# The opening of a transformer block on one core: operand fills taken one by one, the second batch's normalised rows written by ScalarE, and the first slots' order written as a list

## The reference

```python
mod = (_silu(L0_c) @ L0_wmod).reshape(8, 6, 1, -1)      # sa, ca, ga, sb, cb, gb
ga, gb = sign(.) * maximum(abs(.), 0.25)
h = _layernorm(x) * (1 + ca) + sa
x = x + ga * attention(h)        # softmax(q k^T / 4) v, then wo, with biases
h = _layernorm(x) * (1 + cb) + sb
x = x + gb * ffn(h)              # shared: gelu(h up) down; routed: the same, times the gate of the top 4 of 16
```

## Time and profile before

| | us |
|---|---|
| median of 3 runs | 888.06 |
| lowest, highest | 887.6, 888.15 |
| the profiled execution | 887.85 |
| its span, first to last instruction | 886.1 |
| PE busy | 834.1 (94%) |
| ACT busy | 681.8 (77%) |
| DVE busy | 607.6 (69%) |
| POOL busy | 395.8 (45%) |

### The profile page before, as it was taken

How to read it: one execution, slowest core, us unless ns; L and a number is a source line. 1 busy time by engine, 2 the same in 40 slices (tenths; PEclk the granted TensorE clock), 3 DMA queues, 4 the chain that set the end, 5 groups by cost and what they waited for, 6 DMA issues and landing times.

```text
span 886.1 us, 19423 instructions
## 1 busy us (share of the span) xinstructions
PE 834.1 (94%) x7652; PEld 450.5 (51%) x7652; DVE 607.6 (69%) x1211; ACT 681.8 (77%) x1158; POOL 395.8 (45%) x349
## 2 busy tenths in 40 slices
PE   5858788999999999999999999999999999998998
PEld 4322133355545575566545655566555554555555
DVE  4675677777688866977588776976687668632452
ACT  5468878878997789878988889878987788855452
POOL 4365215224744255335633464426623263346472
PEclk9987889899999999999999999999999999999999
DMA  7024400344025221424025402431314300330140
GB/s 259 13 75 131 137 13 14 97 127 138 13 61 175 90 61 52 148 62 138 25 68 169 138 2 73 154 100 25 105 48 149 119 2 1 133 120 1 61 163 26
DMA packets 47290, 77.18 MB, mean 87 GB/s; under 512 B 6392, under 2 KB 41432, under 8 KB 43104
## 3 DMA queue, kind: packets, MB, share of 16 engines
q1 hardware_dynamic: 47200, 75.94, 27.1%
HBM read 63.47 MB, written 12.34 MB: 86 GB/s over the span
## 4 chain that ended last, share of the span: by engine, by line
PE 74%; ACT 9%; DVE 8%; POOL 4%; issue 3%; DMA 0%; ACTq 0%; DVEq 0%
PE scalar_bank L950 21%; PE down_bank L1118 18%; PE vector_bank L1026 9%; PE scalar_bank L1009 6%; PE vector_bank L1009 6%; PE vector_bank L950 5%; DVE neg_max L907 3%; PE scalar_bank L1038 3%; ACT q_aug L701 2%; ACT probs L715 2%; PE vector_bank L1050 2%; ACT rows L684 1%; DVE gelu L894 1%; ACT f_ring L673 1%; PE scalar_bank L1062 1%
## 5 line engine op out<-in xcount | busy, mean ns | idle before, releaser
L907 DVE TENSOR_REDUCE neg_max<-vector_bank 128x1 f16<-128x512 f32 x484 | 306.7, 686 | 84.9 <-PE vector_bank L1009 75.6
L715 ACT ACTIVATE probs<-scalar_bank 128x512 f32<-128x512 f32 x486 | 262.3, 605 | 41.9 <-PE scalar_bank L1009 39.2
L651 POOL TENSOR_TENSOR act_lo<-gelu,act_hi 128x512 f16<-128x512 f32 x144 | 172.7, 1217 | 164.9 <-ACT act_hi L692 146.8
L1118 PE MATMUL down_bank<-down_hi,act_hi 64*128 64x256 f16 x1120 | 174.8, 271 | 0.4 <-PE down_bank L1118 0.2
L1118 PE MATMUL down_bank<-down_lo,act_hi 64*128 64x256 f16 x1120 | 173.7, 269 | 0.0
L1118 PE MATMUL down_bank<-down_hi,act_lo 64*128 64x256 f16 x1120 | 173.7, 269 | 0.0
L1009 PE MATMUL vector_bank<-k_aug,q_aug 64*128 64x512 f16 x484 | 132.9, 393 | 13.9 <-ACT q_aug L701 7.4
L894 DVE TENSOR_TENSOR gelu<-gelu,gates 128x512 f32<-128x512 f32 x128 | 110.3, 882 | 47.7 <-ACT gelu L750 47.4
L1009 PE MATMUL scalar_bank<-q_aug,k_aug 64*128 64x512 f16 x486 | 126.3, 389 | 3.9 <-ACT probs L715 1.7
L750 ACT ACTIVATE gelu<-scalar_bank 128x512 f32<-128x512 f32 x144 | 85.0, 596 | 57.6 <-PE scalar_bank L950 39.0
L1026 PE MATMUL vector_bank<-probs,v_aug 128*32 128x512 f32 x992 | 117.0, 601 | 0.0
(11 more groups left out here) (200 smaller groups left out, 1255.2 us busy)
## 6 DMA issues: line engine op xcount, KB each, us to landing
gates<-gates_by_expert SPq DMA_DIRECT2D x32, 1024.0 KB, 5.2
q_aug<-q_parts SPq DMA_DIRECT2D x90, 64.0 KB, 2.7
k_aug<-k_parts SPq DMA_DIRECT2D x90, 64.0 KB, 3.1
x_pre<-in_x SPq DMA_DIRECT2D x8, 512.0 KB, 4.6
x_post<-in_x SPq DMA_DIRECT2D x8, 512.0 KB, 6.5
out<-x_post SPq DMA_DIRECT2D x16, 256.0 KB, 3.6
gates<-in_w_up SPq DMA_DIRECT2D x4, 576.0 KB, 11.2
gates<-in_w_down SPq DMA_DIRECT2D x4, 576.0 KB, 4.5
```

What stands on the lines that cost most here:

```text
L651: pool.tensor_tensor(act[1][:, c, :], gelu[:, n % NGELU, :], act[0][:, c, :], ALU.subtract).then_inc(s_elo, 1)
L715: scalar.activation(probs[:, n % U, :], src[:], ACT.Exp, scale=SCALE).then_inc(taken[kind], 1)
L907: dve.tensor_reduce(neg_max[:, (u // 2) % TT, at:at + 1], src[:], AX.X, ALU.max, negate=True).then_inc(done, 1)
L1118: ins = pe.matmul(o, act[a][at:at + 64, act_slot(b, c), tok:tok + P], wd[w][at:at + 64, c, :], start=n == 0 and k == 0, stop=c == NEX - 1 ...
```

## The change

Five things change.

1. `fill` becomes three items. `("fill", 0)` fills `q_aug[1]`, `("fill", 1)` `k_aug[1]`, `("fill", 2)` `v_aug[1]`. The fill of `v_aug[0]` goes into POOL's setup behind that of `k_aug[0]` and counts on `s_aug0`. The waits follow: the first batch's `qk_in` and `v` wait for `s_aug0` at 3 alone, the second batch's `qk_in`, `no_max` and `v` for `s_aug1` at 3.
2. The second batch's `rows1` moves from DVE to ACT: four activations with scale and bias. The bias (minus mean times the reciprocal deviation) is made by two more small instructions on POOL in `stats1`, with a semaphore `s_bias1` of its own.
3. `late` on DVE is cut in two: the weight split stays, the modulations and gates become an item `gm`.
4. The first 459 items of the list are written out in `BEGIN`, up to the maxima of the ninth slot; the rest keeps its order. The last 2222 items are the same in both lists. In `BEGIN` many of the pairs of `max` and `exp` are parted.
5. Within that, `mods` moves on SP from behind the first `qk_in` to the very front of the list, ahead of the second batch's `x_pre`. `gb` moves ahead by 17 places of SP's stream and `wsplit` 5 goes from ahead of `qk` (0, 1) to behind `pv` (2, 0).

```diff
+BEGIN = [("h1T", 0, 0, 0), ("mods", 0, 0, 0), ("h1T", 0, 1, 1), ("first", 0, 0, 0), ("x_pre", 1, 0, 0), ("first", 0,
+    1, 1), ("qk_out", 0, 2, 2), ("first", 0, 2, 3), ("max", 0, 0, 2), ("qk_out", 0, 3, 3), ("first", 0, 4, 4), ("max",
+    0, 3, 9), ("late", 0, 0, 0), ("qk_in", 0, 2, 2), ("max", 0, 10, 10), ("qk_in", 0, 3, 3), ("max", 0, 11, 11),
+    ("first", 0, 5, 5), ("stage", 0, 3, 3), ("qk", 0, 2, 2), ("gm", 0, 0, 0), ("max", 0, 12, 15), ("first", 0, 6, 6),
+    ("maxT", 0, 0, 0), ("qk", 0, 3, 3), ("max", 0, 16, 16), ("stage", 0, 4, 5), ("stats1", 1, 0, 0), ("max", 0, 17,
+    18), ("first", 0, 7, 7), ("exp", 0, 0, 1), ("max", 0, 19, 19), ("exp", 0, 2, 2), ("max", 0, 20, 21), ("fill", 0,
+    0, 0), ("max", 0, 22, 22), ("exp", 0, 3, 3), ("v", 0, 0, 0), ("wsplit", 0, 0, 0), ("exp", 0, 4, 4), ("v", 0, 1,
+    1), ("wsplit", 0, 1, 1), ("rows1", 1, 0, 0), ("exp", 0, 5, 5), ("max", 0, 23, 24), ("fill", 0, 1, 1), ("max", 0,
+    25, 25), ("stage", 0, 6, 6), ("exp", 0, 6, 6), ("max", 0, 26, 26), ("wsplit", 0, 2, 2), ("h1T", 1, 0, 0), ("exp",
+    0, 7, 7), ("max", 0, 27, 30), ("h1T", 1, 1, 1), ("exp", 0, 8, 8), ("wsplit", 0, 3, 3), ("qk_out", 1, 0, 0),
+    ("max", 0, 31, 31), ("maxT", 0, 1, 1), ("exp", 0, 9, 9), ("wsplit", 0, 4, 4), ("max", 0, 32, 32), ("exp", 0, 10,
...
+    begin = [(kind, n, b) for kind, b, first, last in BEGIN for n in range(first, last + 1)]
+    placed = set(begin)
+    return begin + [item for item in HEAD + parted([item for _, _, item in sorted(spots)]) if item not in placed]
...
                     if n == (2 if b == 0 else 0) and b < 2:
-                        sp.wait_ge(s_aug0, 2)
-                        sp.wait_ge(s_aug1, 4)
+                        sp.wait_ge((s_aug0, s_aug1)[b], 3)
...
+            pool.memset(v_aug[0][:], 1.0).then_inc(s_aug0, 1)
...
                 if kind == "fill":
-                    pool.memset(q_aug[1][:].bitcast(U32), 0).then_inc(s_aug1, 1)
-                    pool.memset(k_aug[1][:].bitcast(U32), 0x3C003C00).then_inc(s_aug1, 1)
-                    for m in v_aug:
-                        pool.memset(m[:], 1.0).then_inc(s_aug1, 1)
+                    dst, value = ((q_aug[1][:].bitcast(U32), 0), (k_aug[1][:].bitcast(U32), 0x3C003C00), (v_aug[1][:], 1.0))[n]
+                    pool.memset(dst, value).then_inc(s_aug1, 1)
...
                     power(b, mv[0], rstd[0], s_ln1, s_rs1)
+                    if b == 1:
+                        mean, var = mv[0][:, :, 0], mv[0][:, :, 1]
+                        pool.tensor_scalar(var, mean, -1.0, None, ALU.mult).then_inc(s_bias1, 1)
+                        pool.wait_ge(s_bias1, 1)
+                        pool.wait_ge(s_rs1, 4)
+                        pool.tensor_tensor(var, var, rstd[0][:], ALU.mult).then_inc(s_bias1, 1)
...
+                elif kind == "rows1" and b == 1:
+                    scalar.wait_ge(s_bias1, 2)
+                    wait(scalar, made["h1T"], 2, b, 0)
+                    for t in range(TT):
+                        scalar.activation(rows1[:, t, :], x_pre[:, t, :], ACT.Identity, bias=mv[0][:, t, 1:2],
+                                          scale=rstd[0][:, t:t + 1]).then_inc(s_ln1, 1)
...
                     w4_lo(1)
+                elif kind == "gm":
                     dve.wait_ge(s_setup_mm, 2)
...
-                elif kind == "rows1" and b > 0:
+                elif kind == "rows1" and b > 1:
...
-                        dve.wait_ge(s_aug1, 4)
+                        dve.wait_ge(s_aug0, 3)
+                        if b > 0:
+                            dve.wait_ge(s_aug1, 3)
```

More of the change, by code:

```diff
@@ L101 @@
 HEAD = [("x_pre", 0, 1), ("h1T", 0, 0), ("h1T", 1, 0), ("first", 0, 0), ("first", 1, 0), ("first", 2, 0), ("first", 3, 0)]
-EARLY = {("late", 0): 4.47, ("fill", 0): 14.82, ("first", 4): 3.2, ("first", 5): 5.04, ("first", 6): 9.23, ("first",
-    7): 16.56, ("qk", 2): 6.68, ("qk_out", 2): -4.56, ("qk", 3): 12.18, ("qk_out", 3): -1.18, ("qk_in", 2): 2.91,
-    ("qk_in", 3): 6.45, ("v", 0): 22.33, ("v", 1): 24.2, ("wsplit", 0): 22.13, ("wsplit", 1): 29.84, ("wsplit", 2):
-    32.78, ("mods", 0): 5.13, ("stage", 3): 3.59, ("stage", 4): 18.1, ("stage", 5): 29.04}
+EARLY = {("late", 0): 4.47, ("first", 4): 3.2, ("first", 5): 5.04, ("first", 6): 9.23, ("first", 7): 16.56, ("qk", 2): 6.68, ("qk_out", 2): -4.56, ("qk", 3): 12.18, ("qk_out", 3): -1.18, ("qk_in", 2): 2.91, ("qk_in", 3): 6.45, ("v", 0): 22.33, ("v", 1): 24.2, ("wsplit", 0): 22.13, ("wsplit", 1): 29.84, ("wsplit", 2): 32.78, ("mods", 0): 5.13, ("stage", 3): 3.59, ("stage", 4): 18.1, ("stage", 5): 29.04, ("fill", 0): 14.82, ("fill", 1): 17.82, ("fill", 2): 22.82, ("gm", 0): 6.47}
 SPLITS = [(0, 3), (0, 7), (0, 11), (2, 11), (3, 9)]
@@ L260, in plan @@
         slot(g, lambda place, *items: put(g, place, *items))
-    return HEAD + parted([item for _, _, item in sorted(spots)])
+    begin = [(kind, n, b) for kind, b, first, last in BEGIN for n in range(first, last + 1)]
+    placed = set(begin)
+    return begin + [item for item in HEAD + parted([item for _, _, item in sorted(spots)]) if item not in placed]
 PLAN = plan()
@@ L427, in block_kernel @@
         s_ln1, s_ln2 = sem("ln1_steps"), sem("ln2_steps")
+        s_bias1 = sem("second_ln1_bias")
         s_rs1, s_rs2 = sem("rstd1_steps"), sem("rstd2_steps")
```

50 lines of the change are left out of this document (added).

## The result

The changed kernel takes 891.56 us (median of 7 runs, 890.24 to 892.78) against 888.15: a ratio of 1.0035, 95% interval 1.0024 to 1.0046. It is slower by a third of a per cent where 1.0% faster was forecast. (888.15 is a median of seven too; one of those seven took 1640.13 us, far from every other run here.) Its profiled execution took 891.04 us with a span of 889.3 us, against 886.1 us of span before.

What follows compares the result with a forecast made beforehand. PE was taken as the bound, busy nearly throughout, so opening gains pass through as a shift. Head 6.1, setup 0.3, (a) 1.4 and (b) 1.2 make 9.0 us off 887.85: 879.0 us as median, range 869 to 886.

Steps and rivals of the forecast that it cites:

- Fills: Four POOL fills (5.49 us) leave the way ahead of the second batch's power; POOL has room, the `v` wait goes.
- Rows by ACT: Second batch's normalised rows move from DVE (4.19 us there) to ACT, at 2.35 us for four.
- The head, 6.1 us: Stretch from 47.40 us: ACT reaches `qk` (0, 1) at 69.5 instead of 75.65 us; lower bound 3.0 us gained.
- signs of being wrong: ACT waiting for the bias, DVE for `x_pre` at `stats1`, or a mean clock under 0.85 from 80 to 180 us.
- Setup: Opening: fewer maxima ahead of `first` 4 gain 0.3 us (0 to 0.6); two maxima ahead of the gates cost nothing.
- (a): Turn to the second batch: fewer maxima in a row and `exp` products under the wait gain 1.4 us (0 to 2).
- (b): PE's 1.60 us wait for the second norm's rows at 155.47 us shrinks: 1.2 us gained (0 to 1.6).
- (c): Slots around the first batch's `maxT` 2 and other turns: same sum of work and waits, 0 (-2 to +3).
- (d): Two half-clock stretches behind a `maxT`: 5.2 us would go at full clock, but new ones may come; taken as 0.
- Given back later: Rival, 18%: the head gains, but the finer order costs what (a) and (b) were to bring; 882.5 to 886.3 us.
- The clock too: Rival, 24%: shorter waits behind each `maxT` keep the clock full there; 869 to 876.5 us, most likely 874.
- Slower: Rival, 9%: parted `max` and `exp` make PE wait for banks in turn, doubling half-clock time; 891 us.

Runs made afterwards that it cites:

- list_to_second: The changed kernel's list, gates right behind the weight split, only up to the first batch's second `maxT`, old order behind: 881.85 us, ratio 0.9941.
- list_to_fifth: As list_to_second, but with the written-out list kept up to the second batch's first `maxT`: 889.26 us, ratio 1.001.
- fills_only: Old order, fills as single steps behind the second batch's power, gates right behind the weight split, rows still on DVE: 889.66 us, ratio 1.0018.
- gates_back: The changed kernel with one item moved, `gm` right behind `late`, ahead of `max` 10 and 11: 890.43 us, ratio 1.0025.

## Why the prediction was wrong, point by point

**Fills.** The step held for POOL (the `v` wait is gone, the fills found room), but alone it brought nothing, since DVE's rows then met the moved fill and the weight split.

**Rows by ACT.** Right, with its price: 2.06 us against 2.35. It carries the head.

**The head, 6.1 us.** The term was right in size and was reached only without the late gates: ACT came to `qk` (0, 1) 5.7 us earlier in list_to_second. In the changed kernel it came at 74.29, 1.4 us earlier, and the transposes at 60.12, not at 55 to 57. The load of `x_pre` was in time, and of the signs of being wrong that were named none came: the clock from 80 to 180 us was 0.93, not under 0.85.

**Setup.** The step that failed first: "its chain from 34.95 on holds the same instructions, so nothing". The same instructions in another order were not nothing. Two maxima went first, 1.9 us; the gates were then held beside POOL, 1.9 us; the four maxima behind the gates came late, and PE, which is in order, waited for them with a `first` product and the transposes of `maxT` 0 queued behind, and lost its clock. I had placed the gates' end at about 39 us; it was 42.4. Cost: 4.2 us at the first copies, 2.1 (the clock fell on `v` in both profiles) to 3.7 us (in neither) at the second.

**(a)** Right in size: 1.4 us alone against before, 0.95 us against slot C of list_to_second (15.29 to 14.34 us). But the clock then fell on the `v` products and took 2 us.

**(b)** Right: 1.2 forecast, 1.0 measured alone, the wait 0.34 us after.

**(c)** The step that failed most. "The same sum of work and of waits": 0, with -2 to +3. In the changed kernel it was a loss of 1.8 us in A and B (3.2 in list_to_fifth), 2.7 in D (5.6 alone), 1.6 in F and G. The sum of PE's work is not the same, because the score products had run two at a time: 159 turns for 132, and some 7.7 us more of PE's work over the eight slots. The code's `64 * (u % 2)` and the even pairs of the old list would have told it, and so would a look at the starts in PE's timeline. I had read only durations.

**(d)** Left at 0. In the whole the clock was better in the profile after (24.1 us at half clock instead of 37.6), but that paid for most of PE's added work only. Its place changes from execution to execution.

**The rivals.** "Given back later" has the right shape, with the ends set too near, as it let the small steps lose no more than (a) and (b) were to bring; its 882.5 to 886.3 do not even follow from the 3 to 6 us that it names, which give 882 to 885. "The clock too" came true by itself without its result. "Slower" had the right sign and time (891 us) by another mechanism: 14 us more of half clock were its condition, and there were 13 us less; what cost was PE's own work and the gates. It is in single slots (A, D) that a parted order and more half clock came together as it said; its waits did not, for PE's idle time there hardly changed. Its 9% were too few, for its mechanism was one of several by which a list of 460 places, each argued only at the few that looked bad, could lose.

The forecast was 9.0 us gained and 3.2 were lost in the profiled execution. Of the 12.2 us between, 4.5 are the setup (4.2 lost for 0.3 gained), none the head (6.1 in H, as forecast), 6.2 the slots A to G (3.6 lost where (a) and (b) were to gain 2.6), and 1.5 the late dip of the clock, of which the forecast had nothing.

By the experiments, the accounts close at the ninth copies: -5.6 for the list up to the second slot, +3.7 late gates, +1.8 for A and B, -1.6 for C, +2.7 for D, -0.9 for E, +1.6 for F and G give +1.7. These are leads of single profiles, with the chance said above. D of the changed kernel can be held against D of list_to_second, at nearly the same clock (0.92 and 0.91): of its 2.75 us more, 1.46 are PE busy (17.33 for 15.87) and 1.29 PE idle, beside waits of ACT for single products (seven, of 0.45 to 1.35 us each, between 122 and 133 us). No kernel was run that restores the pairs within the new slots, so that the parted pairs are the cause of PE's added work is argued from the starts, the count and the busy time, not shown by an experiment.

## What to carry to other kernels

Before reordering small products, look at their starts as well as their durations: two that start together share the array, and moving one away can be new work for PE. Moving a step behind another one costs what that one waits, even if the set of instructions is the same. And try a written order slot by slot: here the first 80 items were worth 0.6%, and the 380 behind them, with the gates moved late, lost more than that.

## What the runs showed of the hardware

A fill by POOL, which only writes, held up DVE's `tensor_scalar` until it was over: in fills_only a row of 0.40 us took 1.33 us beside the fill of `k_aug`, and the next 3.43 us beside a weight split and a fill. In the setup the same befell a `scalar_tensor_tensor` (1.66 instead of 0.68 us) and a cast (1.12 instead of 0.16), beside POOL's additions. ACT's same four rows stood at 2.06 to 2.09 us beside anything. The page "SBUF — State Buffer" of the Trainium skill, section "Who interferes with whom", has the rule; these rows agree with it, and I had applied it to the rows alone and not to the gates.

The granted clock of one stretch differed between executions of one kernel (0.27 or 0.42 us for the same `v` product), and with it the total by 2.4 us. A shift of 0.1 to 0.4 us ahead of it went with it: `v` products at half clock came in gates_back, whose copies stood 0.14 us later than in list_to_fifth with the same list, and at full clock there. That the shift is the cause is not shown.
